# Attention values gathered and divided without transposes, context tiles turned beside the value tiles

## The reference

```python
x = x + attention(layernorm(x), ctx, ctx)        # 16 heads of 16, biases on q, k, v and o
#   q = xn @ Wq.T + bq ; k = ctx @ Wk.T + bk ; v = ctx @ Wv.T + bv
#   out = softmax(q k.T / 4) v, heads side by side, then out @ Wo.T + bo
x = x + ffn(layernorm(x))
#   gate = fp4(x) @ fp4(w_gate).T ; up = fp4(x) @ fp4(w_up).T      (256 -> 704)
#   y = fp4(silu(gate) * up) @ fp4(w_down).T                       (704 -> 256)
#   fp4: blocks of 16 are scaled by max/6, rounded to an 8-value grid and scaled back
```

## Time and profile before

| what | value |
|---|---|
| median of 3 executions | 1804.34 us (1802.04 to 1804.83) |
| the profiled execution | 1801.16 us |
| its span | 1799.4 us |
| TensorE busy | 1687.2 us (94%) |
| VectorE busy | 1398.6 us (78%) |
| ScalarE busy | 1155.4 us (64%) |
| GpSimd busy | 528.4 us (29%) |
| granted TensorE clock, mean | 0.984 |

### The profile page before, as it was taken

One profiled execution on the slowest core, in us unless ns is written; L12 is line 12 of the kernel. 1 busy time (PEld: TensorE's weight loads), 2 busy tenths in 40 slices (PEclk: granted clock), 3 DMA queues, 4 the chain that ended last, 5 costly groups with the idle time before them and its releaser, 6 DMA issues.

```text
span 1799.4 us, 26659 instructions
## 1 busy us (share of the span) xinstructions
PE 1687.2 (94%) x9600; PEld 658.4 (37%) x9600; DVE 1398.6 (78%) x1969; ACT 1155.4 (64%) x2335; POOL 528.4 (29%) x409
## 2 busy tenths in 40 slices
PE   3799789999999999999999999999999999989978
PEld 2332124333343343433443333433334334423425
DVE  6777887888868887788878888688877887688538
ACT  2366567776667666776667766676667766666651
POOL 4316340442107320152204421073201622012213
PEclk8899999999999999999999999999999999999989
DMA  6643432142323322043221423243220422300000
GB/s 147 151 77 92 90 77 37 47 116 38 55 37 96 91 49 50 13 110 73 55 52 44 118 40 55 37 96 90 50 48 12 108 40 43 52 1 1 7 18 12
DMA packets 98031, 109.09 MB, mean 61 GB/s; under 512 B 18788, under 2 KB 83308, under 8 KB 97900
## 3 DMA queue, kind: packets, MB, share of 16 engines
q1 hardware_dynamic: 93344, 103.26, 27.1%
q10 hardware_dynamic: 4556, 4.13, 1.1%
HBM read 76.78 MB, written 30.16 MB: 59 GB/s over the span
## 4 chain that ended last, share of the span: by engine, by line
PE 74%; DVE 15%; ACT 7%; issue 3%; DMA 1%; ACTq 0%; POOL 0%; SPq 0%; DVEq 0%; POOLq 0%
PE pvb L714 19%; PE st L685 18%; PE mx L699 9%; PE misc L632 7%; DVE cmx L941 6%; PE misc L582 5%; ACT prob L870 4%; PE misc L589 4%; PE misc L644 2%; PE misc L652 2%; PE misc L521 1%; PE misc L640 1%; PE misc L611 1%; PE misc L570 1%; PE misc L559 1%
## 5 line engine op out<-in xcount | busy, mean ns | idle before, releaser
L870 ACT ACTIVATE prob<-st 128x512 f32<-128x512 f32 x1630 | 887.6, 599 | 419.9 <-PE st L685 418.2
L941 DVE TENSOR_REDUCE cmx<-mx 128x2 f32<-128x1024 f32 x768 | 905.3, 1219 | 215.4 <-PE mx L699 211.7
L685 PE MATMUL st<-qstack,kstack 112*128 112x512 bf16 x1630 | 520.6, 386 | 32.6 <-ACT prob L870 20.0
L714 PE MATMUL pvb<-prob,vv 128*17 128x512 f32 (+1 forms) x3328 | 440.7, 601 | 0.6 <-ACT prob L870 0.6
L685 PEld LDWEIGHTS st<-qstack,kstack 112*128 112x128 bf16 x1630 | 128.4, 98 | 554.9 <-issue 315.7
L699 PE MATMUL mx<-kstack,qstack 48*128 48x512 bf16 (+1 forms) x2048 | 253.3, 336 | 32.8 <-DMA qstack<-scr_q 16.3
L1202 POOL TENSOR_TENSOR cin<-cin 128x400 f32<-128x400 f32 (+1 forms) x60 | 55.3, 922 | 418.6 <-ACT cin L798 418.6
L1235 POOL TENSOR_TENSOR ht<-ht,rh 128x704 f32<-128x704 f32 x29 | 40.2, 1385 | 425.0 <-DVE rh L917 425.0
L632 PE MATMUL misc<-wguT,rowsT 128*128 128x352 f32 x456 | 154.9, 462 | 0.0
L699 PEld LDWEIGHTS mx<-kstack,qstack 48*128 48x128 bf16 x2048 | 58.0, 94 | 195.7 <-issue 147.2
L632 PEld LDWEIGHTS misc<-wguT,rowsT 128*128 128x128 f32 x456 | 87.1, 191 | 41.4 <-issue 1.0
(11 more groups left out here) (201 smaller groups left out, 1593.3 us busy)
## 6 DMA issues: line engine op xcount, KB each, us to landing
kstack<-scr_k SPq DMA_DIRECT2D x384, 100.1 KB, 4.3
scr_k<-cin SPq DMA_DIRECT2D x48, 300.0 KB, 3.2
qstack<-scr_q SPq DMA_DIRECT2D x372, 32.0 KB, 1.9
cin<-ctx_in SPq DMA_DIRECT2D x8, 1280.0 KB, 6.6
scr_q<-qp SPq DMA_DIRECT2D x15, 384.0 KB, 5.4
scr_k<-cin SPq DMA_DIRECT2D x16, 300.8 KB, 4.4
xn<-x SPq DMA_DIRECT2D x8, 512.0 KB, 3.9
x<-x SPq DMA_DIRECT2D x8, 512.0 KB, 3.8
```

The source lines that it names most:

```text
L685: mm(score_bank(it, n, pair, h)[0:KROWS[kt], :], kstack[:, hd, KOFF[kt]:KOFF[kt] + KROWS[kt]], qstack[:, hd, :], start=True, stop=True).th ...
L714: last = mm(pvb[32 * h:32 * h + D + 1, :], vv[0:w, kt, HG * g + h, :], prob[0:w, n % 2, h, :], start=(kt == 0), stop=(kt == NKT - 1))
L870: activate(prob[0:KROWS[kt], n % 2, 2 * pair + h, :], score_bank(it, n, pair, h)[0:KROWS[kt], :], ACT.Exp, scale=SCALE).then_inc(exp_done[ ...
L941: v.tensor_reduce(cmx[:, g % 2, h0:h0 + 2, at:at + 1], products, op=ALU.max, axis=AX.X).then_inc(max_free, 1)
```

## The change

- Weights of the value matmul are 32 columns instead of 17: `vv` holds, for each two heads, 16 columns of values, 16 ones, 16 values, so each head's slice gives its 16 values and 16 copies of its sum.
- `pvT`, `attT` and the copies behind them are gone. SyncE moves the 4 heads' values of a group from `pvs` to `att` and their sums to `sums` with 8 transfers of 16 partitions x 2 KB (in the tail 4 from SyncE and 4 from ScalarE). `att` is already turned, so `o` reads it.
- VectorE divides 128 x 128 tiles: a reciprocal and a multiply in each of 8 entries "values" per batch, at steps 29, 30, 32, 36 and, for the second half, at 2, 3, 4, 5 of the next iteration. `o` job 0 waits for the first two of the second half, job 1 for all four.
- Context tiles are turned one at a time (2 transposes) directly behind a `v` job, in the other half of its bank, by the "next" batch in steps 42 to 51 and by "early" in 0 to 4. The next job waits for the readers of both. The prologue and the first iteration keep pairs (`ctx2`).
- `xnT` goes to steps 7 and 8, `xqT` both to 19, key job 7 from 19 to 18, query job 0 and key job 2 change places. On GpSimd the split of query job 1 goes behind the rounding of `x` and key job 5; the bias of `x1` waits until value tile 9 has been read (step 1).
- `xnT` shares memory with `mt`, `bvl` with `rowsT`; hence two waits for the queries.

The diff, cut to its core (the memory declarations and the parts for the first iteration are left out; the plain renames too):

```diff
@@ SLOTS, DVE_EXTRA, POOL_WORK
-    0: ([("v", 8, "att")], [("ctxT", 0, "early")]),
-    1: ([("v", 9, "att")], [("pvT", 3, "late")]),
-    2: ([("v", 10, "att")], [("attT", 0, "late")]),
-    3: ([("v", 11, "att")], [("attT", 1, "late")]),
-    4: ([("v", 12, "att")], [("ctxT", 1, "early")]),
-    5: ([("o", 0, "late")], [("ctxT", 2, "early")]),
-    6: ([("o", 1, "late")], [("ctxT", 3, "early")]),
-    7: ([("ctxT", 4, "early")], [("ctxT", 5, "early")]),
-    8: ([("ctxT", 6, "early")], [("xnT", 0, "early")]),
-    9: ([("k", 0, "early")], [("xnT", 1, "early")]),
+    0: ([("v", 8, "att")], [("ctx2", 0, "once")]),
+    1: ([("v", 9, "att")], [("ctx2", 1, "once")]),
+    2: ([("v", 10, "att")], [("ctx2", 2, "once")]),
+    3: ([("v", 11, "att")], [("ctx2", 3, "once")]),
+    4: ([("v", 12, "att")], []),
+    5: ([("o", 0, "late")], []),
+    6: ([("o", 1, "late")], []),
+    7: ([("xnT", 0, "early")], []),
+    8: ([("xnT", 1, "early")], []),
+    9: ([("k", 0, "early")], []),
-    11: ([("k", 2, "early")], []),
-    12: ([("q", 0, "early")], []),
+    11: ([("q", 0, "early")], []),
+    12: ([("k", 2, "early")], []),
-    18: ([("pvT", 0, "att")], [("xqT", 0, "late")]),
-    19: ([("k", 7, "early")], [("xqT", 1, "late")]),
+    18: ([("k", 7, "early")], []),
+    19: ([("xqT", 0, "late")], [("xqT", 1, "late")]),
-    31: ([("gate", 5, "late")], [("pvT", 1, "att")]),
+    31: ([("gate", 5, "late")], []),
-    41: ([("down", 2, "late")], [("pvT", 2, "att")]),
+    41: ([("down", 2, "late")], []),
...
-    1: [("late", "norm", 3)], 5: [("late", "stats", 0)], ... 19: [("att", "norm", 0)],
-    31: [("att", "norm", 1)], ... 42: [("att", "norm", 2)],
+    2: [("late", "values", 4)], 3: [("late", "values", 5)], 4: [("late", "values", 6)], 5: [("late", "values", 7), ("late", "stats", 0)],
+    29: [("att", "values", 0)], 30: [("att", "values", 1)], 32: [("att", "values", 2)], ... 36: [("att", "values", 3)],
...
-    16: [("early", "q", 1), ("late", "xround", 0)], 17: [("early", "k", 5)], 18: [("early", "k", 6)], 20: [("early", "k", 7)],
+    16: [("late", "xround", 0)], 17: [("early", "k", 5), ("early", "q", 1)], 18: [("early", "k", 6)], 19: [("early", "k", 7)],
@@ SyncE
+            def values_in(it, g, part):
+                sp.wait_ge(pvs_done, it.count(part, NG, g + 1))
+                c, s = divmod(g, 2)
...
+                for h in range(HG):
+                    row = HALF * s + D * h
+                    values, weights = 2 * D * h + D * (h % 2), 2 * D * h + D * (1 - h % 2)
+                    sp.dma_start(att[row:row + D, c, :], pvs[values:values + D, :]).then_inc(values_row[g], 16)
+                    if it.kind != "tail":
+                        sp.dma_start(sums[row:row + D, :], pvs[weights:weights + D, :]).then_inc(values_row[g], 16)
@@ SyncE, body: values_in(3, "late") is first; values_in(0) before queries_in(0, "early"),
@@ values_in(1) after ctx_in_rows, values_in(2) after x_in
@@ TensorE
                     elif kind == "o":
+                        pe.wait_ge(att_ready, c(NC2 * QT, QT + 2 * j + 2))
...
+                    if guest(it, job):
+                        context_tile(guest(it, job))
+                def context_tile(job):
+                    _, j, part = job
...
+                    w, o = KROWS[j], job_bank(it, job)
+                    for h in range(NC2):
+                        last = turn(o[:, h * 128:h * 128 + w], ctx_rows[0:w, j, h * 128:(h + 1) * 128], ident[0:w, 0:w])
+                    last.then_inc(full["ctxT"], 1)
-                        last = mm(pvb[32 * h:32 * h + D + 1, :], vv[0:w, kt, HG * g + h, :], prob[0:w, n % 2, h, :], ...)
+                        last = mm(pvb[2 * D * h:2 * D * (h + 1), :], vv[0:w, kt, (HG * g + h) // 2, D * (h % 2):D * (h % 2 + 2)], prob[0:w, n % 2, h, :], ...)
@@ ScalarE
+                    elif kind == "ctxT":
+                        act.wait_ge(full["v"], c(NKT, j + 1 - NKT))
+                        w = KROWS[j]
+                        last = copy(ctxT[:, :, KOFF[j]:KOFF[j] + w], src.rearrange("p (c n) -> p c n", c=NC2)[:, :, 0:w])
@@ VectorE
+                def values_divided(part, n):
+                    c, t = divmod(n, QT)
+                    cols = slice(128 * t, 128 * (t + 1))
+                    if t == 0:
+                        for g in (2 * c, 2 * c + 1):
+                            dve.wait_ge(values_row[g], it.count(part, 128, 128))
+                    v.reciprocal(sums[:, cols], sums[:, cols]).then_inc(rec_ready, 1)
+                    dve.wait_ge(rec_ready, it.count(part, NC2 * QT, n + 1))
+                    v.tensor_tensor(att[:, c, cols], att[:, c, cols], sums[:, cols], ALU.mult).then_inc(att_ready, 1)
@@ GpSimd, bias
+                        if it.kind != "tail":
+                            pool.wait_ge(free["v"], it.count("att", NKT, 10))
```

More of the change, by code:

```diff
@@ L123 @@
 PRE_SLOTS = {
-    5: ([("ctxT", j, "early") for j in range(7)], []),
+    5: ([("ctx2", j, "early") for j in range(7)], []),
     8: ([("xnT", j, "early") for j in range(2)], []),
@@ L173 @@
 TAIL_EXTRA = {
-    1: DVE_EXTRA[1], 3: [("late", "half", 0)], 4: [("late", "half", 1)], 6: [("late", "hscale", 0)],
+    1: [("late", "values", p) for p in range(4, 8)], 3: [("late", "half", 0)], 4: [("late", "half", 1)], 6: [("late", "hscale", 0)],
     7: [("late", "hpower", 0), ("late", "hscale", 1), ("late", "hpower", 1)], 9: [("late", "hscale", 2), ("late", "hpower", 2)],
@@ L333, in job_count, with tiles_turned, guest @@
         def job_count(it, job):
-            return it.count(job[2], PER[job[0]], job[1] + 1)
+            kind, j, part = job
+            if kind == "ctx2":
+                return (PAIRS if part == "once" else 0) + j + 1
+            if part == "once":
+                return j + 1
+            if kind == "ctxT":
+                return tiles_turned(it, part, j + 1)
+            return it.count(part, PER[kind], j + 1)
+        def tiles_turned(it, part, k):
+            return (it.batch(part) - 2) * NKT + NKT - 8 + k
+        def guest(it, job):
+            if job[0] != "v" or it.kind == "pre":
+                return None
+            part = {"early": "next", "att": "early"}[job[2]]
+            return ("ctxT", job[1], part) if part in it.parts else None
         def job_bank(it, job):
+            if job[0] == "ctxT":
+                return misc[:, 2 * 128:]
             b = BANKS.bank(it.kind, job)
@@ L873, in group_out @@
                     act.wait_ge(pv_done, it.count(part, STEPS, NKT * (g + 1)))
-                    if g:
-                        act.wait_ge(full["pvT"], it.count(part, NG, g))
+                    need(act, values_row[(g - 1) % NG], it.count(part, 128, 128 if g else 0))
                     copy(pvs[:, :], pvb[:, :]).then_inc(pvs_done, 1)
+                    if it.kind == "tail":
+                        act.wait_ge(pvs_done, it.count(part, NG, NG))
+                        for h in range(HG):
+                            row, weights = HALF + D * h, 2 * D * h + D * (1 - h % 2)
+                            act.dma_start(sums[row:row + D, :], pvs[weights:weights + D, :]).then_inc(values_row[g], 16)
                 has_att, has_late = "att" in it.parts, "late" in it.parts
```

136 lines of the change are left out of this document (73 added, 63 removed).

## The result

The changed kernel takes 1790.38 us (median of 4 runs, 1788.38 to 1791.45), against 1803.89 for the kernel before, run beside it (4 runs). The ratio is 0.9927, 95% interval 0.9914 to 0.994: 13.5 us or 0.7% faster. The forecast was 4.7 us faster, 1799.6; the measured time lies on the lower edge of the range that it gave itself (1790 to 1808).

The account below looks back on a forecast made before the run. TensorE was taken to bound the kernel (74% of the span). Per loop iteration -7.4 + 5.7 + 0.5 = -1.2 us, six times -7.2; with the other iterations and tail -4.7, giving 1799.6 us; range 1790 to 1808, with rivals 1776 to 1817.

Parts of the forecast that it names:

- rival A: Stalls at `o` 1 and key job 7 not paid in full: 28 us less, 1772; one of them about 1786; chance 0.27.
- What goes: Per loop iteration, removed transposes, cheaper context tiles, waits beside them and the moved bias: together -7.4 us.
- The excess of step 49 over 3.47: Bias of `x1` on GpSimd meets the split of the maxima, VectorE late; its move taken as 0.7 us gained per iteration.
- Step 6: `o` 1 waits for division entry 7, which stands behind both maxima of step 5: stall 2.1 us, step near 6.3.
- Step 18: ScalarE, reading key job 7, waits for GpSimd's split of key job 5 behind the rounding of `x`: stall 2.2 us.
- Step 32: `hqT` 2 waits 0.3 us, after the step 29 entry meets GpSimd's rounding of `h`.
- Step 37: Entry in step 36 delays the reader of `gate` 7 and so `hqT` 4: stall 1.15 us, step near 5.7.
- Wider weights: Longer weight loads in the value matmuls, 32 columns for 17: 0.01 us a step, 0.5 per iteration.
- B: Rival, slower: weight loads serial and in front, 0.10 us a step, 1838; a third exposed 1809; chance 0.18.
- C: Rival: rows land after 4.3 us instead of 1.9, VectorE waits 1.2 us in step 2: 1808; chance 0.12.
- Tail: After the last copy, issues, landing and four entries delay the read of `o` 0 to 1745.1 from 1741.35: +3.8 us.
- First iteration: Loses early turned jobs, gets pairs in steps 0 to 3: 0, within 4 either way, +0.5 us for its weights.

## Why the prediction was right, and where not

The sign was right, the size a third of what came; the 1790.38 is nearer to rival A with one of its two stalls gone (about 1786) than to the 1799.6. By its own steps:

- **What goes.** The turned jobs were priced right: steps 0 to 5, 7, 8, 9, 31 and 41 lost 0.47 to 0.85 us each. A pair with the wider weights was taken at 0.20 and costs 0.12: 13 x 0.08 = 1.0 us an iteration more gain. The excess of step 49 over 3.47 was 0.85 in the mean of six and is gone, for 0.7; the bias alone accounts for 0.4 of it by its run, what took the rest away is not shown. The waits beside the removed jobs, outside steps 18 and 19, gave back 0.5 an iteration (0.26 each in steps 9 and 31) where 1.0 was said. The 3.84 us for step 14 should be 3.79, which changes nothing.
- **Step 6.** "TensorE hears of it at about 528.3. Stall: 2.1 us" held: the wait is 1.98, and steps of 6.45 us stand where 6.3 was said. What it missed is the clock after the wait: 1.6 us in five iterations, 8 us.
- **Step 18: the step that failed.** "That rounding starts at 572.48, when VectorE is ready, and nothing in the change makes it earlier." The change did: VectorE was ready late because the power operation took 1528 ns beside the query split, and GpSimd itself was busy with that split until 571.85; the split now runs later, and both hold-ups, some 0.6 us each, go. "Moving query job 1 behind this doesn't shorten it" fell with it. Steps 18 and 19 are 9.02 and not 10.0, 1 us less in each of six iterations. Undoing this one move costs 8.5 us (6 x 1.21 of it in step 18) and brings back the wait of 2.2. Rival A had this possibility in it ("VectorE's chain has less under it"), without its cause.
- **Step 32** was to lose 0.3 and lost nothing. **Step 37** was right (5.63 for 5.69), and so was the price of an entry (0.94 + 0.29 for 0.96 + 0.28).
- **Wider weights**: 0.013 us a step for 0.01. B is out by a run. C is out by the trace: the rows of group 3 are on time.
- **Tail**: +3.8 was said, +5.8 is there. The landing came 0.7 later. The rest of that term was built wrongly: it let `o` 0 be read after four entries (4.9 us) and gave its matmuls no time. `o` 0 waits for two (2.6), and its matmuls take 3.5 at half the clock. **First iteration**: 0.5 was said and -2.5 came, within the 4 either way; the start came out 1.2 longer, which is not explained.

Sum of the misses in the profiled execution, rounded: step 18 -6, pairs and weights -6, step 32 -2, step 49 -1, first iteration -3, last iteration -1 are -19; the halved clock +8, the smaller waits +3, tail +2, start +1, the rest of step 6 +1 are +15. That leaves -4; the measured miss is -10.3 - (-4.7) = -5.6, so the account is good to 2 us. Errors of some size stood against each other: that the total came within the range is in part luck. The medians differ by 3.2 us more than the profiled executions, and no step stands for these; the profiled execution of the kernel before, 1801.16, was shorter than its median of 1803.89.

## What to carry to other kernels

Before pricing an edit as "nothing makes it earlier", look at the shortest and the longest duration of every operation on that chain: a 694 beside a 1528 says that a neighbour is charging it, and moving the neighbour is part of the change. When work moves onto an engine that runs in the order written, lay each new entry over the reader that stands behind it and find the one that another engine waits for; here moving that one job by one step gave more (23.6 us) than the whole change (13.5). And try a move per kind of iteration: entry 3 in step 38 gains in the loop and loses in the first iteration, where the clock halves behind it.

## What was not expected of the hardware

A wait of 2 us on TensorE, in a stretch where it is otherwise busy for 97% of the time, was followed by 3.4 us at a granted clock of 0.50 in five of seven cases, and cost 3.6 us instead of 2. The two kernels that lack only that wait had the full clock from 240 us to 1690 us, although waits of 1.0 and 1.2 us stayed in their steps 18 and 37. With a wait of 2.2 us in step 18 as well, the halved stretch came there in the loops and no longer after the one in step 6. And a wait of 0.83 us in the first iteration was followed by 6.8 us at 0.50 when entry 3 stood in step 38. What decides between the cases wasn't found.
